# The end of a segment softmax in a graph-network kernel: scaling on ScalarE, comparisons behind the gathers, a later second sum

## The reference

```python
h = jnp.maximum(_layernorm(x), 0.0)
msg = relu(h[src] + edge_attr)                 # 25000 x 256
p = msg @ W_fc.T + b_fc
scores = p @ Q.T                               # 4 heads
w = exp(scores - segment_max(scores, dst)[dst])
alpha = w / maximum(segment_sum(w, dst)[dst], 1e-9)
pooled = [segment_sum(alpha[:, h:h+1] * p, dst) for h in range(4)]
mean_p = segment_sum(p, dst) / maximum(deg, 1)
gate = softmax(mean_p @ Wg.T + bg)             # per node, over heads
out = x + sigmoid(einsum('nh,nht->nt', gate, pooled))
```

## Time and profile before

| what | us |
|---|---|
| median of 3 runs | 657.8 (657.22 to 658.36) |
| the profiled execution | 653.36 |
| its span | 651.3 |
| edge stage, to the last eviction | about 280 |
| softmax end, to `c_ready` | to 312.4 |
| steps and output | to the end |

### The profile page before, as it was taken

How to read it: one execution, slowest core, us unless ns; L and a number is a source line. 1 busy time by engine, 2 the same in 40 slices (tenths; PEclk the granted TensorE clock), 3 DMA queues, 4 the chain that set the end, 5 groups by cost and what they waited for, 6 DMA issues and landing times.

```text
span 651.3 us, 12707 instructions
## 1 busy us (share of the span) xinstructions
PE 543.0 (83%) x2670; PEld 439.9 (68%) x2671; DVE 462.0 (71%) x1607; ACT 416.3 (64%) x765; POOL 454.9 (70%) x342
## 2 busy tenths in 40 slices
PE   2799999999999999920899989878878876878775
PEld 2588888888887778810687768666666665656554
DVE  3986878998999998779776667555646555456454
ACT  1667778888897888723035556656665665666674
POOL 6777777777777777107045677787887878778784
PEclk9998999999999999975799999999999999899999
DMA  8566666766668899530289999999999999999999
GB/s 206 165 198 166 201 194 211 219 203 204 197 189 284 295 300 315 181 129 1 72 285 350 386 345 320 320 331 351 312 318 326 354 314 334 318 304 348 327 342 324
DMA packets 137275, 171.54 MB, mean 263 GB/s; under 512 B 10132, under 2 KB 123820, under 8 KB 137238
## 3 DMA queue, kind: packets, MB, share of 16 engines
q10 hardware_dynamic: 91344, 90.23, 42.3%
q1 hardware_dynamic: 33046, 42.70, 20.6%
q0 software_dynamic: 12848, 38.20, 18.5%
HBM read 111.50 MB, written 59.60 MB: 263 GB/s over the span
## 4 chain that ended last, share of the span: by engine, by line
PE 54%; DVE 15%; ACT 9%; issue 8%; POOL 4%; ACTq 3%; DVEq 3%; DMA 3%; POOLq 0%; SPq 0%
PE bank L803 22%; PE bank L895 22%; PE bank L788 5%; ACT arena L649 4%; POOL arena L516 4%; DVE spread L1406 4%; ACT bank L625 3%; PE bank L800 3%; DVE stats L1214 2%; ACTq L652 2%; DVEq L1410 1%; DMA p_keep<-in_x_dram,idx 1%; DVE arena L1220 1%; DVEq L1406 1%; DMA arena<-in_x_dram 1%
## 5 line engine op out<-in xcount | busy, mean ns | idle before, releaser
L895 PE MATMUL bank<-p_keep,spread 128*128 x1172 | 274.5, 388 | 54.3 <-DVE spread L1406 43.4
L895 PEld LDWEIGHTS bank<-p_keep,spread 128*128 128x128 f32 x1172 | 218.7, 192 | 110.9 <-issue 83.7
L1406 DVE TENSOR_SCALAR spread<-bank,rel,wgt 128x128 f32<-128x128 f32 x586 | 195.6, 403 | 131.4 <-PE bank L895 82.2
L516 POOL TENSOR_TENSOR arena<-arena 128x1024 f32<-128x1024 f32 x96 | 224.9, 2353 | 74.9 <-ACT arena L649 74.3
L803 PE MATMUL bank<-w_all,arena 128*128 128x264 f32 (+1 forms) x784 | 208.8, 389 | 0.0
L649 ACT ACTIVATE arena<-bank 128x1024 f32<-128x1024 f32 x97 | 99.3, 1023 | 139.7 <-PE bank L895 130.7
L479 POOL DMA_INDIRECT p_keep<-in_x_dram,idx x124 | 124.5, 1004 | 38.8 <-issue 31.4
L803 PEld LDWEIGHTS bank<-w_all,arena 128*128 128x128 f32 (+1 forms) x784 | 135.3, 192 | 15.8
L625 ACT ACTIVATE bank<-zero 128x1024 f32<-128x1024 f32 x98 | 100.5, 1026 | 3.0
L543 ACT ACTIVATE arena<-bank 128x256 f32<-128x256 f32 x196 | 74.2, 379 | 33.2 <-PE bank L788 32.6
L479 POOL DMA_INDIRECT arena<-in_x_dram,idx x72 | 73.5, 1020 | 23.1 <-issue 14.9
(11 more groups left out here) (248 smaller groups left out, 239.5 us busy)
## 6 DMA issues: line engine op xcount, KB each, us to landing
out_dram<-arena ACTq DMA_DIRECT2D x97, 512.0 KB, 4.4
arena<-in_x_dram ACTq DMA_DIRECT2D x73, 512.0 KB, 5.3
arena<-in_edge_attr_dram SPq DMA_DIRECT2D x48, 512.0 KB
arena<-in_x_dram POOLq DMA_DIRECT2D x24, 512.0 KB, 5.6
p_spill<-p_keep SPq DMA_DIRECT2D x16, 512.0 KB, 3.9
p_keep<-p_spill SPq DMA_DIRECT2D x16, 512.0 KB, 5.0
p_keep<-in_x_dram,idx POOLq DMA_INDIRECT x124, 2.8
arena<-in_x_dram,idx POOLq DMA_INDIRECT x72, 5.0
```

The lines of the kernel that those rows point to most:

```text
L516: pool.tensor_tensor(yout[:, slot, :, :], yout[:, slot, :, :], xin[:, slot, :, :], ALU.add).then_inc(summed, 1)
L895: nc.tensor.matmul(places[:, bass.ds(place, T)], spread[:, k0 + k, :], p_rows[:, bass.ds(p_at, T)], start=False, stop=True, skip_group_che ...
L1406: v.tensor_scalar(spread[:, k, :], bank[:, 7, P:2 * P], rel[:, bass.ds(s0 + k, 1)], wgt[:, bass.ds(s0 + k, 1)], ALU.is_equal, ALU.mult).th ...
```

## The change

1. ACT makes all four products of w with `gain` (two blocks, two sides), one instruction for each head, each with a per-partition scale read from memory: 16 instructions between the load of the sigmoid table and the three clears. DVE adds the four heads of each in pairs. `tot` and `wa`, `top` and `wb` take the results.
2. POOL compares all steps with the tile number right after its last gather, in four instructions. The results of steps 0 to 127 go to `ones` and `column`, those of the later steps to `sel_late` in the arena. POOL no longer makes sums behind `gain_ready`.
3. DVE loads the first two words of `needs_of` in its edge loop at k = 167, after a wait on `words_in`, instead of behind `c_ready`.
4. The second part of the sum (458 steps wide) moves behind step 11: PE issues it after the first 12 steps, and DVE copies it to `wgt` after the spreads of steps 12 to 23.

```diff
+            pool.wait_ge(rows_copied, PARTS + 2)
+            pool.wait_ge(a_step, A_STEPS)
+            pool.wait_ge(node_step, 23)
+            for b in range(BLK):
+                n, tile_no = ROWS[b], tile_f[0:ROWS[b], b:b + 1]
+                pool.tensor_scalar(sel_early[b][0:n], step_tile[0:n, 0:P], tile_no, None, ALU.is_equal).then_inc(selected, 1)
+                pool.tensor_scalar(sel_late[0:n, b, :], step_tile[0:n, P:STEPS], tile_no, None, ALU.is_equal
+                                   ).then_inc(selected, 1)
...
-            pool.wait_ge(rows_copied, PARTS + 2)
-            pool.wait_ge(chain_turned, 2)
-            for b in range(BLK):
-                pool.tensor_scalar(sel_1[:, b, :], step_tile[:, :], tile_f[:, b:b + 1], None, ALU.is_equal
-                                   ).then_inc(selected, 1)
-            pool.wait_ge(gain_ready, 1)
-            for b, w, to in ((0, wa, a1), (1, wb, top)):
-                n = ROWS[b]
-                gain_of = gain[0:n, b, 0, :].unsqueeze(2).broadcast_to([n, H, P])
-                pool.tensor_tensor(to[0:n], w[0:n], gain_of, ALU.mult).then_inc(by_first_done, 1)
-                pool.wait_ge(by_first_done, 3 * b + 1)
-                pool.tensor_tensor(to[0:n, 0:2, :], to[0:n, 0:2, :], to[0:n, 2:4, :], ALU.add).then_inc(by_first_done, 1)
-                pool.wait_ge(by_first_done, 3 * b + 2)
-                pool.tensor_tensor(to[0:n, 0, :], to[0:n, 0, :], to[0:n, 1, :], ALU.add).then_inc(by_first_done, 1)
...
             nc.scalar.activation(eps[:, 0:1], zero[:, 0:1], ACT.Sigmoid)
+            act.wait_ge(gain_ready, 1)
+            for b, w, by_first in ((0, wa, tot), (1, wb, top)):
+                for side, to in ((0, by_first), (1, w)):
+                    n = ROWS[b]
+                    for h in range(H):
+                        last = nc.scalar.activation(to[0:n, h, :], w[0:n, h, :], ACT.Copy, scale=gain[0:n, b, side, h:h + 1])
+                    last.then_inc(gained, 1)
             act.wait_ge(rows_read, 1)
             for z in range(SLOTS):
                 clear(z)
...
+            sum_weights(bank[:, 7, 2 * P:3 * P], lambda b: sel_early[b])
...
             steps(0, 0, 0, HALF, 1)
             steps(1, 0, HALF, HALF)
-            with pe.Fori(1, TURNS) as turn:
+            sum_weights(bank[:, 6, 0:later_steps], lambda b: sel_late[:, b, :])
+            for h in range(2):
+                steps(2 + h, AHEAD, h * HALF, HALF)
+            with pe.Fori(2, TURNS) as turn:
...
+                if k == ROWS[0] + 71:
+                    assert a_ops[0] == A_STEPS
+                    dve.wait_ge(words_in, 64)
+                    first, second = need_word(0), need_word(1)
...
-            blocks = ((0, ROWS[0], wa, total_a, last_a, a1), (1, ROWS[1], wb, total_b, last_b, top))
-            for h in range(H):
-                for b, m, w, total, by_last, by_first in blocks:
-                    w_of, g_of, to = w[0:m, h, :], gain[0:m, b, 1, h:h + 1], by_last[0:m]
-                    if h == 0:
-                        ins = v.tensor_scalar(to, w_of, g_of, None, ALU.mult)
-                    else:
-                        ins = v.scalar_tensor_tensor(to, w_of, g_of, to, ALU.mult, ALU.add)
-                then(ins)
+            blocks = ((0, ROWS[0], total_a, tot, wa), (1, ROWS[1], total_b, top, wb))
+            for b, m, total, by_first, by_last in blocks:
+                for side, part in ((0, by_first), (1, by_last)):
+                    dve.wait_ge(gained, 2 * b + side + 1)
+                    ins = v.tensor_tensor(part[0:m, 0:2, :], part[0:m, 0:2, :], part[0:m, 2:4, :], ALU.add)
+            then(ins)
+            for b, m, total, by_first, by_last in blocks:
+                for part in (by_first, by_last):
+                    v.tensor_tensor(part[0:m, 0, :], part[0:m, 0, :], part[0:m, 1, :], ALU.add)
...
             spreads(0, HALF, HALF)
+            for h in range(2):
+                need(2 + h)
+                spreads(AHEAD, h * HALF, HALF)
             dve.wait_ge(wgt_summed, 2)
-            then(v.tensor_copy(wgt[:, P:STEPS], bank[:, 6, 0:STEPS - P]))
-            with dve.Fori(1, TURNS) as turn:
+            then(v.tensor_copy(wgt[:, P:STEPS], bank[:, 6, 0:later_steps]))
+            with dve.Fori(2, TURNS) as turn:
```

## The result

| | before | changed |
|---|---|---|
| median of 6 runs, us | 656.71 (654.93 to 658.36) | 649.67 (646.60 to 652.57) |
| ratio, 95% interval | | 0.9895 (0.9858 to 0.9932) |
| profiled execution, span | 653.36, 651.3 | 652.05, 650.4 |

The forecast was 655.9, 1.9 us less, with a range from 653.0 to 658.8. The measured time is 7.0 less. The changed kernel was timed three more times, on three different chips: 0.9925 (0.9897 to 0.9953), 0.9948 (0.9914 to 0.9982), 0.9903 (0.9867 to 0.9940). Weighted by their intervals the four give 0.9920 +- 0.0017, that is 5.3 +- 1.1 us less. The first result stands at the far end of this.

What follows compares the result with a forecast made beforehand. The softmax end, a serial chain on VectorE then TensorE, was taken to delay everything behind it. Comparisons 1.9 + products 0.7 - second sum 0.5 - edge stage 0.2 = 1.9 us less: 655.9, range 653.0 to 658.8.

Steps and rivals of the forecast that it cites:

- Comparisons, 1.9: Softmax end: moving GpSimd's comparisons away frees 1.90 us in VectorE's chain, bounds 1.30 to 2.24; edge stage loses 0.1.
- The three named operations: VectorE's L1354, L1356 and L1346, beside GpSimd's comparisons, said to lose 0.79, 0.51 and 0.60 us to them.
- Products, 0.7: From `gain_ready` to `c_ready`: 7.7 us instead of 8.36, with ScalarE's 16 products 0.30 apart; 0.7 saved.
- Words: Two register loads moved into the edge loop: first spread 0.5 us sooner, edge stage loses 0.1, bounds 0 to 1.5.
- Second sum, 0.5 lost: Behind `c_ready`: step 0 1.85 us earlier, but TensorE stands 1.0 us; 0.5 lost, bounds 1.6 lost to 1.85 gained.
- the late rise that was forecast as the bad case: Behind `c_ready`: if the clock rises 2.15 us later, another 1.07 us goes, 1.6 lost for the second sum.
- - 0.2 (edge stage): Edge stage: 0.1 us lost to the moved comparisons and 0.1 to the early register loads.
- I subtract the same 1.9: Runs lie 4.4 us above the profiled execution; the gain of 1.9 us forecast there was taken off them too, giving 655.9.
- the early first step is kept: Rival, steps to end: DMA sets the end, all 1.85 us of the second sum's move arrive; 653.6 us, chance 0.17.
- ScalarE's products don't overlap: Rival, `gain_ready` to `c_ready`: 0.9 us lost instead of 0.7 gained; 657.5 us, chance 0.14.
- the loads hold up the edge stage: Rival, edge stage: TensorE has no reserve, the addition behind the loads comes 1.5 us late; about 657.3 us, chance 0.10.
- The low clock lasts: Rival, behind `c_ready`: TensorE's gap delays the clock's rise to `c_ready` + 12, 3.2 us lost; 658.6 us, chance 0.12.

## Why the prediction was wrong

Step by step, by its own terms:

- **Comparisons, 1.9.** Measured 1.95 (22.92 to 20.97), but the agreement is in part luck. The three named operations gave back 2.27, not 1.90: all 0.93 of L1346 went, also the part put down to GpSimd's L491, "which stays" (its successor now ends 0.6 us before that operation starts). Against this stand 0.31 net lost because GpSimd now gets in ahead of L1357, which the forecast did not hold. And two thirds of the term are the form of the comparisons, not their place. Cost in the edge stage none that shows, 0.1 was taken.
- **Products, 0.7.** Measured 0.83 against the trace used, and 1.3 against the executions of before in which GpSimd gets in first. 7.7 from `gain_ready` to `c_ready` was forecast, 7.53 measured; start to start 0.30 forecast, 0.29 measured.
- **Words.** 0.1 lost in the edge stage: PE's turns there are 1.30 and 1.27 apart once instead of 1.22, which is 0.13. The first spread is 0.46 earlier (0.5 forecast).
- **Second sum, 0.5 lost.** Step 0 at 2.48 behind `c_ready` (2.35 forecast), with the gap of 1 us. The low clock lasted to 7.8 to 8.5 behind `c_ready` in four traces, against 5.3 to 6.6 in four of before: near the late rise that was forecast as the bad case. The first sigmoid is 1.6 later. At the end runs give 0.4 us for the move with an interval of 1.8 to either side. The sign is not settled.

Up to `c_ready` the mechanism was right and the sum nearly so: 2.6 forecast, 3.0 in the traces, and the runs with these two parts alone say 3.0 +- 1.1. **The step that failed is the other half of the sum, "- 0.5 (second sum, with the copy's 0.5 in it)" and the 0.1 for the loads in "- 0.2 (edge stage)".** It made the moved sum and the early loads a loss of 0.6 us together. The runs show a gain: 2.3 +- 1.6 us by the pooled ratios (5.3 against 3.0). A least squares fit of the 278 executions without extra matmuls, each part a term of its own and each comparison with its own level, says the same with less noise:

| part | forecast | traces | fit of the runs |
|---|---|---|---|
| comparisons, form and place | 1.9 | 1.95 | 2.0 +- 1.2 |
| products | 0.7 | 0.83 or 1.3 | 1.1 +- 1.1 |
| loads early | lost 0.1, the copy's gain of 0.5 in the next row | step 0 0.46 earlier | 1.7 +- 1.3 |
| second sum late | lost 0.5, the copy's 0.5 in it | first sigmoid 1.6 later | lost 0.2 +- 1.0 |
| loads and second sum together | lost 0.6 | about 0.2 gained outside the span | 1.5 +- 1.2 |
| all | 1.9 | 3.0, and 0.4 outside the span | 4.6 +- 0.8 |

The first row of the fit also holds whatever the new buffers and code do by themselves. Of the whole, 3.0 us stand in the traces and 0.4 outside the span; another 1.2 by the fit, or 1.9 by the pooled ratios, stay open. The loads are the term that they point at. Where a gain of theirs beyond 0.46 us would come from is not shown: 0.46 is all that the traces have up to step 0, it is also the lower end of the fit's interval, and the edge stage ends at the same time with early loads and with late ones (means 282.1). Seventeen traces can't show a microsecond in a stretch that scatters by 2.5.

Two things more failed. **The range** was built from bounds of single terms on one trace; its lower end lay 4.8 us below the median of before, and the measured median lies 3.3 below that end. It held nothing for the scatter between executions, which with six runs on each side is 2.4 us in the ratio's own interval; three runs within 1.1 us of each other made before look far steadier than it is. And **"I subtract the same 1.9"** took a term read on one execution for the difference of medians. By that the 0.43 us outside the span were put at nothing without a reason, and about 1.7 of the 7.0 us measured first are scatter, since four results say 5.3.

Of the rivals, "the early first step is kept" named the size best (653.6) and is not supported: undoing the move costs nothing measurable. "ScalarE's products don't overlap" and "the loads hold up the edge stage" are refuted by rows. "The low clock lasts" was right in that the rise comes later, but it comes by 8.5 us and not 12, and the price of 3.2 us is not seen.

The Trainium skill (SBUF — State Buffer, "SBUF: two separate sides") says that when a VectorE operation with two SBUF inputs meets a GpSimd operation that reads SBUF, the one that starts first has the shared pair of ports for its whole instruction and the other fully blocks. That fits better than I weighed it for L1399 at 302.14 beside L510 at 302.13: 1.18 us, where it takes 0.29 alone, against GpSimd's 1.04. For the comparisons the recorded span is longer than the block: L1353 takes its usual 0.20 us inside one.

## What to carry to other kernels

Cut each trace at the signals between stages before you compare: a serial stretch repeats to hundredths of a microsecond, and the scatter sits elsewhere. Then build the range from two parts, the bounds of the terms and the scatter of the executions, and take more than three runs as the level of a kernel. Compare device time with span as well: a version can gain outside the trace. When an operation moves on one engine, look for every pair that starts at the same moment on the two engines that get in each other's way, not only for the pair that you mean to part. Where TensorE waits for a serial stretch, matmuls that keep its clock up can be worth more than an earlier first step: the two sums ran in 2.25 us instead of 4.24, and 2.2 +- 2.0 us arrived, where the earlier first step gave nothing measurable. They have to reach close enough: with 3.17 us of idle ahead the clock fell.

## What was not expected of the hardware

- Two executions of one program can take two paths through the same race between VectorE and GpSimd: 8.35 or 8.83 us, nothing between, in four traces of before. Both engines pay: the sum of 128 columns takes 1.18 us instead of 0.29 when GpSimd gets in first, GpSimd's product 1.19 instead of 1.04 when VectorE does.
- Moving the comparisons some 30 us ahead turned another such race over, in every trace: 0.69 and 2.05 us became 1.15 and 1.49.
- With a first sum of four records, about 1 us of idle and then steady steps the clock (1.2 GHz at its low level, 2.4 at its high) rose 6.2 to 8.5 us behind `c_ready` in seven traces; with both sums and the steps behind them without a gap, 4.8 to 6.8 in ten. The two ranges overlap. With matmuls ending 1.16 and 1.90 us ahead of the first sum it did not fall at all; with 3.17 us of idle ahead it fell before the sum began, and 1 us of idle stood behind it too.
